# Conditional LoRA and paged attention in one kernel: a reordered prologue, and the last unit's probabilities transposed on TensorE

## What is computed

```python
w = weight[adapter_ids]; x = x + einsum('bsi,boi->bso', x, w)     # layer 0, per row
q, k, v = x @ Wq.T, x @ Wk.T, x @ Wv.T                            # 32, 8 and 8 heads of 128
q, k = rope(rmsnorm(q)), rope(rmsnorm(k))
k_all, v_all = concat(cache[block_table], new), 512 + 128 keys
probs = softmax(q @ k_all.T / sqrt(128), cached keys masked beyond cache_seqlens)
x = x + (probs @ v_all) @ Wo.T
```

## Time and profile before

| | us |
|---|---|
| median of 3 runs | 1047.99 (1045.32 to 1051.49) |
| the profiled execution | 1052.44 |
| its span in the trace | 1050.6 |
| TensorE busy in the span | 1013.0 (96%) |
| mean granted TensorE clock | 0.99 of full |

### The profile page before, as it was taken

How to read it: one execution, slowest core, us unless ns; L and a number is a source line. 1 busy time by engine, 2 the same in 40 slices (tenths; PEclk the granted TensorE clock), 3 DMA queues, 4 the chain that set the end, 5 groups by cost and what they waited for, 6 DMA issues and landing times.

```text
span 1050.6 us, 19559 instructions
## 1 busy us (share of the span) xinstructions
PE 1013.0 (96%) x5500; PEld 871.0 (83%) x5500; DVE 854.9 (81%) x1778; ACT 803.0 (76%) x2094; POOL 787.0 (75%) x807
## 2 busy tenths in 40 slices
PE   7789999999999999999999999999999999999996
PEld 5567878888888888888888888888888888888884
DVE  6556657666888898988989998898999989998893
ACT  4245546665788888898889888988888878988883
POOL 1767767565587978888888967888888968888663
PEclk9889999999999999999999999999999999999999
DMA  6679988888589889797888897798788988787874
GB/s 212 189 216 284 286 248 225 230 235 208 90 158 164 147 158 165 144 174 139 157 157 159 159 156 160 145 172 149 153 158 157 160 151 160 150 172 130 156 146 108
DMA packets 477501, 180.85 MB, mean 172 GB/s; under 512 B 420417, under 2 KB 457426, under 8 KB 475346
## 3 DMA queue, kind: packets, MB, share of 16 engines
q1 hardware_dynamic: 372480, 150.57, 68.8%
q10 hardware_dynamic: 103890, 26.94, 11.8%
q0 software_dynamic: 1024, 2.10, 0.7%
HBM read 109.25 MB, written 35.66 MB: 138 GB/s over the span
## 4 chain that ended last, share of the span: by engine, by line
PE 80%; SPq 4%; DVE 4%; ACT 3%; DMA 3%; POOL 3%; issue 3%; ACTq 0%; POOLq 0%; DVEq 0%
PE S L1226 19%; PE O L1159 6%; PE O L1161 6%; PE O L1160 6%; PE Q L1159 5%; PE Y L1159 5%; PE Q L1161 5%; PE Q L1160 5%; PE Y L1160 5%; PE Y L1161 5%; PE T L1165 4%; PE KV L1160 2%; PE KV L1161 2%; PE KV L1159 2%; SPq L394 2%
## 5 line engine op out<-in xcount | busy, mean ns | idle before, releaser
L945 DVE SCALAR_TENSOR_TENSOR pr<-pr,rc,raw 128x640 f16<-128x640 f32 x208 | 237.2, 1141 | 22.1 <-ACT raw L723 16.7
L925 DVE CUSTOM_DVE_ANT_0 pr<-S,mask,rst 128x640 f32<-128x640 f32 x256 | 225.3, 880 | 32.1 <-PE S L1226 27.8
L738 ACT ACTIVATE pr<-pr,nb 128x640 f32<-128x640 f32 x256 | 211.6, 827 | 25.1 <-DVE nb L925 25.1
L723 ACT ACTIVATE raw<-pr,rc 128x640 f16<-128x640 f32 x208 | 166.3, 825 | 3.2 <-DVE rc L941 2.9
L540 POOL TENSOR_TENSOR m<-m 128x512 f32<-128x512 f32 x64 | 111.3, 1739 | 71.3 <-DVE m L973 68.6
L494 POOL TENSOR_TENSOR kl<-raw,kh 128x512 fp32r<-128x512 f32 x64 | 96.6, 1509 | 47.8 <-ACT kh L622 47.2
L1226 PE MATMUL S<-kh,qh 128*128 128x320 f32 x512 | 121.4, 318 | 7.1 <-DVE nb L925 6.4
L682 ACT ACTIVATE Q<-Q 128x128 f32<-128x128 f32 x256 | 68.2, 267 | 73.5 <-DVE m L973 73.5
L515 POOL TENSOR_SCALAR ptl<-first 128x512 fp32r<-128x512 f16 x130 | 103.1, 793 | 23.0 <-DMA first<-pr 12.8
L515 POOL TENSOR_SCALAR ptl<-turned 128x512 fp32r<-128x512 f16 x130 | 102.8, 790 | 20.5 <-DMA turned<-pr 10.4
L1226 PE MATMUL S<-kh,ql 128*128 128x320 f32 x512 | 116.8, 309 | 0.0
(11 more groups left out here) (114 smaller groups left out, 2694.2 us busy)
## 6 DMA issues: line engine op xcount, KB each, us to landing
cache_rows<-in_kv SPq DMA_DIRECT2D x80, 256.0 KB, 4.9
wraw<-in_wall SPq DMA_DIRECT2D x73, 256.0 KB, 3.2
raw<-cache_rows SPq DMA_DIRECT2D x63, 256.0 KB, 3.2
raw<-cache_rows ACTq DMA_DIRECT2D x49, 256.0 KB, 4.1
cache_rows<-in_kv ACTq DMA_DIRECT2D x48, 256.0 KB
mask<-mask_rows SPq DMA_DIRECT2D x64, 128.0 KB
first<-in_lw SPq DMA_DIRECT2D x6, 1024.0 KB
acc<-in_x SPq DMA_DIRECT2D x8, 256.0 KB
```

The costliest lines, as they stand in the source:

```text
L723: e.activation(upper16[:, g, :], pr[:, slot(u, g), :], ACT.Copy, scale=rc[:, u % 2, g:g + 1]).then_inc(a_f1, 1)
L738: e.activation(pr[:, slot(u, g), :], pr[:, slot(u, g), :], ACT.Exp, bias=nb[:, u % 2, g:g + 1], scale=-1.0, accum_out=sm[:, u % 2, g:g + 1 ...
L925: e.tensor_tensor_reduce(pr[:, slot(u, g), :].rearrange("p (a n) -> p a n", a=2), S[:, :, 0:320], mask[:, u % 2, :].rearrange("p (a n) -> ...
L945: e.scalar_tensor_tensor(out=lower16(u, g), in0=pr[:, slot(u, g), :], scalar=rc[:, u % 2, g:g + 1], in1=upper16[:, g, :], op0=ALU.mult, op ...
```

## The change

In the prologue: 34 warm-up transposes for 44. SP loads row 1 in the middle of unit 0's key pages, and row 2 ahead of the mask; chunk 5 moves to ACT's queue, where all six chunk loads now stand behind the five small loads, and ACT also loads unit 1's first four key pages. POOL issues the four gathers of unit 0 before its loop, as DVE makes the page indices first. Unit 0's keys are split after its queries. L0 of row 1 is computed on PE in period -1, between the projections and turns of unit 0, its sum and transposition come at once, and `project_q(1)` follows two score products of unit 0; the other two are done at the places that they have in all later periods. DVE's four table parts move to the end of period 0. POOL's gathers of unit 1 all come after its `scales(1)`.

In the tail: unit 63's four probability tiles are normalised in place (two on ACT, two on DVE), turned by 20 transposes on PE into banks T, S and S, multiplied into bank Q (not O) and projected into bank KV (not Y). Its planes and its eight DMA transposes are gone, and PE's last part is written out as one list in which the two last units alternate. The semaphores' counts follow.

```diff
-N_WARM = 44
+N_WARM = 34
...
+        def turned_at(u, t):
+
+            if u == LAST:
+                return S[:, t - 2, :] if t in (2, 3) else T[:, t % 2, :]
+            return T[:, T_BANK[t], :]
...
             load_x(0)
-            for t in range(NT):
-                load_kt(0, t)
-            load_w(0, 5)
+            for t in range(2):
+                load_kt(e, kt_regs, 0, t)
+            load_x(1)
+            for t in range(2, NT):
+                load_kt(e, kt_regs, 0, t)
             e.wait_ge(c_rows, 1)
             e.dma_start(mask_rows, mask[0:NB, 1, 0:NT * P]).then_inc(d_rows, 16)
-            load_x(1)
+            load_x(2)
             e.wait_ge(d_rows, 16)
             load_mask(0)
             load_mask(1)
-            for t in range(NT):
-                load_kt(1, t)
-            load_x(2)
+            for t in range(1, NT):
+                load_kt(e, kt_regs, 1, t)
             for c in range(6, NWC):
                 load_w(0, c)
...
+                if i < LAST:
+                    turn_upper(i, 0)
                 if i < NU:
-                    turn_upper(i, 0)
                     load_v(i)
+                if i < LAST:
                     turn_lower(i, 0)
                     turn_upper(i, 1)
...
+            for t in range(NT):
+                gather_v(0, t)
...
-                if 0 < j < NL:
+                if 1 < j < NL:
                     gather_v(j, 0)
                     gather_v(j, 1)
-                keys_lo(j)
+                if i >= 0:
+                    keys_lo(j)
                 split_w(i, 0)
                 q_sum(j)
                 scales(j)
-                if i < 0:
-                    gather_v(0, 0)
-                    gather_v(0, 1)
-                if j < NL:
+                if i == -1:
+                    keys_lo(j)
+                if j == 1:
+                    gather_v(j, 0)
+                    gather_v(j, 1)
+                if 0 < j < NL:
                     gather_v(j, 2)
                     gather_v(j, 3)
...
-                for t in range(3):
-                    p_lo(w, t)
+                if w < LAST:
+                    for t in range(3):
+                        p_lo(w, t)
                 split_w(i, 1)
-                p_lo(w, 3)
-                p_lo(w, 4)
+                if w < LAST:
+                    p_lo(w, 3)
+                    p_lo(w, 4)
...
+                if u < NA or u == LAST:
+                    rounded(pth[:, i % 3, :], turned_at(u, t)).then_inc(a_p, 1)
...
+            def norm_last(g):
+                e.wait_ge(v_rc, 2 * LAST + 1)
+                e.activation(pr[:, slot(LAST, g), :], pr[:, slot(LAST, g), :], ACT.Copy,
+                             scale=rc[:, LAST % 2, g:g + 1]).then_inc(a_norm, 1)
...
-            for c in range(5):
-                e.dma_start(w_raw(0, c), wall[0, :, c * WC:(c + 1) * WC]).then_inc(d_w[c], 16)
...
                             table[g:g + 1, :].broadcast_to([32, NB * NT])).then_inc(d_tab, 16)
+            for c in range(6):
+                e.dma_start(w_raw(0, c), wall[0, :, c * WC:(c + 1) * WC]).then_inc(d_w[c], 16)
...
-            split_chunk(0, 0)
-            split_chunk(0, 1)
...
             e.activation(sn, ang, ACT.Sin).then_inc(c_sin, 1)
             e.wait_ge(c_ang, ANG_COS)
             e.activation(cs, rnd, ACT.Sin).then_inc(c_cos, 1)
+            split_chunk(0, 0)
+            split_chunk(0, 1)
+            l0_hi(0)
+            for c in range(2, 6):
+                split_chunk(0, c)
             e.wait_ge(c_cos, 1)
             e.activation(warmed[:, :], mhalf[:, :], ACT.Exp)
-            split_chunk(0, 2)
-            l0_hi(0)
-            split_chunk(0, 3)
-            split_chunk(0, 4)
-            split_chunk(0, 5)
+            e.wait_ge(d_page, 16)
+            load_kt(e, copy_regs[0:4], 1, 0)
...
                     output_hi(o)
+                if i == 0:
+                    l0_hi(1)
                 if real:
                     exp(i, 0)
                 for place in copied[0:2]:
                     copy_page(*place)
-                if i == 0:
-                    exp(0, 1)
-                    exp(0, 2)
-                keys_hi(j)
-                if i == 0:
-                    l0_hi(1)
-                    exp(0, 3)
+                if i >= 0:
+                    keys_hi(j)
                 if turn:
                     p_hi(w, 0)
...
                 new_v_hi(j)
-                if i > 0:
+                if real:
...
                 q_hi(j)
-                if i > 0:
+                if i == -1:
+                    keys_hi(j)
+                if real:
...
-                output_hi(o)
+                if w != LAST:
+                    output_hi(o)
...
-                if real:
+                if i < LAST:
                     upper_plane(i, 0)
+                elif i == LAST:
+                    norm_last(0)
+                    exp(i, 2)
+                    norm_last(1)
+                    exp(i, 3)
                 if turn:
                     p_hi(w, 0)
+                if w == LAST:
+                    output_hi(w - 1)
+                if turn:
                     p_hi(w, 1)
...
+                if i < LAST:
                     exp(i, 2)
...
+            def norm_last(g):
+                e.wait_ge(v_rc, 2 * LAST + 2)
+                e.tensor_scalar(pr[:, slot(LAST, g), :], pr[:, slot(LAST, g), :],
+                                rc[:, LAST % 2, g:g + 1], None, ALU.mult).then_inc(v_norm, 1)
...
+            key_rows()
+            l0_add(0)
             split_chunk(0, 0)
             split_chunk(0, 1)
+            l0_lo(0)
+            for c in range(2, 6):
+                split_chunk(0, c)
             for part in range(4):
                 rope_part(0, part, 0)
-            l0_add(0)
-            split_chunk(0, 2)
-            l0_lo(0)
-            for c in range(3, 6):
-                split_chunk(0, c)
-            key_rows()
...
                 if i >= 0:
                     largest(i, 0)
                 if i == 0:
-                    for g in range(1, G):
-                        largest(0, g)
-                    l0_add(1)
                     l0_lo(1)
-                    recip(0, slice(0, 3))
-                    recip(0, slice(3, 4))
-                    for part in range(4):
-                        rope_part(1, part, 1)
                 q_products(j)
                 if turn:
                     p_lo(w, 0)
-                if i > 0:
+                if i >= 0:
                     largest(i, 1)
                 if turn:
                     p_lo(w, 1)
...
-                if i > 0:
+                if i >= 0:
                     largest(i, 2)
...
-                if 0 < i < NA:
+                if 0 <= i < NA:
...
-                if i > 0:
+                if i >= 0:
                     largest(i, 3)
...
                 if i == -1:
+                    l0_add(1)
                     rope_part(0, 1, 1)
...
                     scaled_recip(i, 1)
+                if i == 0:
+                    for part in range(4):
+                        rope_part(1, part, 1)
...
                     largest(i, 1)
+                if w == LAST:
+                    p_lo(w, 0)
                 output_lo(o)
+                if w == LAST:
+                    for t in range(1, 5):
+                        p_lo(w, t)
...
+                if i < LAST:
+                    scaled_recip(i, 0)
+                elif i == LAST:
+                    recip(i, slice(0, 2))
                 if real:
...
-                if real:
+                if i < LAST:
                     lower_plane(i, 1)
+                elif i == LAST:
+                    recip(i, slice(2, 4))
+                    norm_last(2)
+                    norm_last(3)
                 add_output(o)
-                if real:
...
+            def turn_last(t):
+                if t == 0:
+                    e.wait_ge(a_norm, 2)
+                    e.wait_ge(v_norm, 2)
+                elif t == 1:
+                    e.wait_ge(v_q, NU)
+                elif t == 2:
+                    e.wait_ge(v_max, 4 * NU)
+                elif t == 4:
+                    e.wait_ge(v_p, 5 * NA + 1)
+                four_turned(turned_at(LAST, t),
+                            [pr[:, slot(LAST, g), t * P:(t + 1) * P] for g in range(G)]
+                            ).then_inc(p_t, 1)
+
...
-                    if u >= 1:
+                    if u == LAST:
+                        e.wait_ge(a_sqq, NU)
+                    elif u >= 1:
                         e.wait_ge(v_o, u)
...
                 if i == 0:
-                    for t in range(3):
-                        l0_part(1, t)
-                        scores(0, t + 1)
-                    l0_part(1, 3)
                     l0_turn(1)
+                    scores(0, 1)
...
                 project_kv(j)
-                if lb == 2:
-                    l0_product(lb)
+                if lb == 1:
```

(75 more changed lines are left out.)

50 lines of the change are left out of this document (28 added, 22 removed).

## The result

Over 20 runs of each kernel the median went from 1048.57 to 1039.95 us, a ratio of 0.992 with a 95% interval of 0.990 to 0.994: 8.6 us less. The forecast was 1035.5 in a range of 1031 to 1043. So the side and the range held, and the size was taken too large: 12.5 where 8.6 came. The forecast's own arm, 1033 to 1038, was missed; the measured median lies 0.55 us from the value of the rival "SP's queue sets the pace", 1040.5. The profiled execution took 1041.16 us, 11.3 less than the profiled 1052.44 of before.

What follows compares the result with a forecast made beforehand. PE, busy 96% of the span, was taken as the bound, with losses in the first 74 us and after the last scores. Prologue -10 and tail -2.5 give -12.5: median 1035.5 us, range 1031 to 1043.

Steps and rivals of the forecast that it cites:

- own arm: Whole kernel: the main forecast, median 1035.5 us with its own range 1033 to 1038, chance 0.60.
- SP's queue sets the pace: Prologue: key pages and loads of rows 3 to 5 come only 5 us earlier, PE waits; 1040.5 us, chance 0.17.
- First scores: Prologue, unit 0: first scores at 26.3 instead of 27.90, 1.6 us sooner; bounds no gain to 2.5.
- wrong: Signs against: waits for early chunks, row 1's matrix or loads at 70 to 110, low clock in row 0's L0, tail norm stop.
- slower: Prologue: row 1's matrix lands late and holds the turn and scores behind L0; 1053 us, chance 0.03.
- `project_q(1)`: Prologue, second row: starts 3.5 us after the first scores, at 29.8 instead of 40.11, 10.3 us earlier.
- `turn_q(2)`: Prologue, PE's next wait, before at 65.76: 53 by POOL's order (-12.7), or 56.3 to 56.5 by the gather (-9.3).
- SP's brake: Prologue: SP's queue gains four pages, chunk 5 and a wait, some 5 us at unit 3, against 10 us key slack.
- Prologue as a whole: All steps up to PE's gapless part: -10 us, ends -5 and -14.
- The clock: Prologue rival: the lower clock behind the stop goes too, -14 there; 1031.5 us in all, chance 0.08.
- Warm-up: Start: ten fewer transposes cost and gain nothing, covered by row 0's matrix load; at most 1.75 us if the clock fell.
- Tail: After the last scores: two PE stops go, 20 transposes add 2.2 us; -2.5 us, ends -1 and -3.5.

Runs made afterwards that it cites:

- the second profile: The unedited kernel before, profiled a second time; that execution took 1053.44 us.
- the run with three edits: Kernel after with mask rows stored early, SP's page copies moved behind row 4's loads, and period 2's weight chunks issued ahead of unit 4's keys; 0.9866 of before.
- the three runs with several edits of SP's list: Kernel after with early mask rows and early weight chunks, plus one of three orders of SP's page copies; 0.9866, 0.9886 and 0.9857 of before.
- the tail alone: Kernel before with only the tail part of the change, without the prologue part; 0.9977 of before, 2.4 us.
- L0 put back: Kernel after with row 1's L0 back between unit 0's score products, period 0's order on PE, DVE and ACT too, queues kept; 0.9970 of before.
- the early chunks alone: Kernel after with period 2's two weight chunks issued ahead of unit 4's 16 key pages on SP; 0.9904 of before.

## Why the forecast was right in side and too large in size

Two chains ran at once: PE's own (L0, scores, projection) and SP's list of loads. The change shortened the first by some 10 us and the second by less than was counted. The range held in part by luck: it was wide enough to take in the rival that the runs bear out.

- **First scores.** Forecast 26.3, measured 24.68: 3.2 us, past the upper bound of 2.5. ACT has no wait for a weight chunk there any more, which was the text's best case. The projections of unit 0 also ran in a window with a granted clock of 0.93 where it was 0.77, but that is the smaller part: the four profiles with the low clock there have 25.29 to 25.55, still ahead of the forecast. PE stopped 0.51 us for row 1's matrix, one of the signs named under "wrong", and not more, so the rival "slower" had no footing.
- **`project_q(1)`.** Forecast 29.8, measured 30.52. One wait was missing in the step: the first `largest` waited 1.59 us for the masks, which SP issued only once the store of the mask rows had landed.
- **`turn_q(2)`.** Forecast 53 or 56.3 to 56.5, measured 56.91. That is near the second value by luck, since that one had PE wait for the gather, and `values_hi(1)` began with no wait for it. POOL's own order came 3.9 us later than worked out (49.86 for 46). ACT's timeline of after, then POOL's:

```profile
35.43 0.63 ACT L650 ACTIVATE kh<-raw 128x512 fp32r<-128x512 f32 x1 [5.77 <-DMA raw<-in_kv]
```

```profile
37.38 1.26 POOL L561 TENSOR_TENSOR m<-m 128x512 f32<-128x512 f32 x1
...
44.29 0.95 POOL L507 DMA_INDIRECT raw<-in_kv,kidx  x1 [0.30 <-issue]
45.29 4.59 POOL L525 TENSOR_SCALAR pr<-pr,rc 128x640 f32<-128x640 f32 x4
49.86 0.62 POOL L546 TENSOR_SCALAR vh<-raw 128x512 fp32r<-128x512 f32 x1
```

  The projection of Q ran at a granted clock of 0.76 in 30 to 40, ACT stood 5.77 us for unit 1's keys, and the four norms took 4.59 us where 3.14 had been counted.
- **SP's brake, the step that failed.** The text gave SP 5 us at unit 3 and set that against 10 us of slack of the keys. In fact unit 3's key pages began at 55.26 on SP's queue where they had begun at 56.40. Row 4's matrix was issued at 70.57 (before 74.20, and 71.42 and 70.22 in the other two profiles with its prologue) and the chunks at 95.38 (99.65, 95.53 and 95.84): up to 4 us sooner than in the first profile, and next to nothing against the other two. The slack of the keys was real, but the matrix and the chunk in the same list had none; the earlier trace rows showed ACT waiting 2.20 us for that very chunk at 110, and the text named it and took -10 all the same. A faster prologue turned a wait of 2.20 (none in the second profile) into one of 3.56 to 10.08. The mechanism of the rival "SP's queue sets the pace" is what happened: it had -5 for the prologue and 1040.5 in all, measured -6.1 and 1039.95. That the loads behind SP's queue are what kept the rest back is shown by the run with three edits, which changes only SP's list (and which pages ACT copies) and gains 5.7. It was given 0.17 and deserved more. Of the signs named under "wrong" this one came too: new waits of ACT, for keys at 71.0 (0.52 us) and for the chunk at 102.5.
- **Prologue as a whole.** -10 forecast, -6.1 measured alone. In the three runs with several edits of SP's list unit 4 came at 109.80 to 110.03, 7.5 to 11.7 us ahead of the three profiles with the prologue of before. So the 10 are about what PE's side can give once SP's list lets it.
- **The clock.** The rival had it come back too. In the profiles it partly did: the shortfall of the granted clock times the window's length adds up to 8.5 us in 16 to 74 before (0.77 and 0.72 of the earlier trace rows, and 0.97 and 0.86 in 30 to 40 and 40 to 52: 13.85 x 0.23 + 10 x 0.03 + 12 x 0.14 + 12 x 0.28), 6.8 in the second profile and 3.4 after (13.85 x 0.07 + 10 x 0.24); an estimate, and an upper one, since PE idles in part of it. Worked out in the same way it is 5.2 for the tail alone, 6.8 with L0 put back, and 0 to 4.4 in the ten profiles with the new prologue. So the clock did come back in part, and its share of the 6.1 us was not separated. The low level is 1.2 GHz, half of the full 2.4. The runs with 44 warm-ups and with the early chunks alone had none in 16 to 74 and were no faster at unit 4 (114.14, 114.42).
- **Warm-up.** Forecast nothing, measured 0.5 us (44 slower) within an interval of +-2.9. L0 of row 0 took 3.67 us in all ten profiles with 34, so the 1.75 us, the price of that L0 at the low level, did not come. But "the cover is that load" held in six of the ten only: in four PE idled 1.38 to 1.63 us before it, and the clock was low at the next step, the projection of unit 0. The first scores came 0.4 to 1.1 us later there, which the wait for the masks took up. The prediction called the cut risky by the Trainium skill, "TensorE: Matmul & The Clock Gate", Part 1 (The HAM clock gate). The traces neither show nor exclude it, since the clock fell at that projection with 44 as well, in two profiles of four.
- **Tail.** -2.5 forecast, -2.4 measured. (42 matmuls at 0.23 are 9.7 and not 9.8, which changes nothing.) 12.4 us were worked out from the restart to the end of the last value product, 12.4 came (1019.34 to 1031.7). The restart, 0.4 and not 0.2 later against PE's place before, is ended by ACT's `p_hi(62, 0)` behind the exps and norms, and by POOL's `p_lo(62)`, which had waited 7.80 us for the lower planes' transposes; the two stops for `output_lo(62)` and for unit 63's transposes are gone.

## What to carry to other kernels

When one engine's chain is shortened by 10 us, ask of every load behind it, one by one, when it is issued and when it is first used: slack of the most frequent load says nothing about the others in the same in-order queue. A wait for a load that does not come sooner itself grows by what is gained ahead of it; one that is already in a trace, however small, is the first to look at. And where a stop only moves one unit on with each repair, open the gates together: each alone measured nothing to 1.7 us here, none clear of its interval of some 3, and the three together 5.7, which is.

## What was not expected of the hardware

- The masks, moved ahead on SP's queue while the DMA engines were 0.93 busy, landed no sooner: issued at 21.52 for 24.12, first used at 28.24 for 27.81. All five profiles with that edit have the first use at 27.76 to 28.84, the five with the same prologue and without it at 27.69 to 28.09, and in all ten it ends a wait for the masks. It is no rule, though: row 4's matrix, issued at 62.78 in the run with three edits and at 70.57 in the kernel after, came in time there, with the DMA engines 0.94 busy in 62 to 74.
- POOL's four norms took 4.59 us beside DVE's table parts and 3.14 without them. DVE's timeline beside them, then the line of the norms (min/median/max in ns of all 48 in the program):

```profile
46.11 3.11 DVE L923 SCALAR_TENSOR_TENSOR tab<-acc 128x384 f32<-128x384 f32 x4
```

```profile
L525 POOL TENSOR_SCALAR pr<-pr,rc x48: 791/802/1562, 45.3 to 251.7; 128x640 f32<-128x640 f32 x48
```

  The four norms beside the table parts took 0.810 us at least, 1.132 in the median and 1.562 at most, where the median of the 48 is 0.802; the four table parts took 0.545 to 1.155 us. The Trainium skill, "SBUF — State Buffer", section "SBUF: two separate sides", says that VectorE and GpSimd take the shared ports exclusively and that the loser waits out the whole instruction. The longest norm is longer by 0.76, which is within the lengths of one table part and agrees with it. But 1.45 us in all is about two table parts (3.11 / 4 = 0.78 in the mean) for four norms, so not each norm waited out a whole part. It goes either way, too: in the ten profiles with the new prologue the norms took 3.44 to 4.60 us and the table parts 2.57 to 3.99, where the norms alone took 3.13 to 3.14 in the four with the old order. In the tail POOL's five `p_lo(62)` took 3.66 us beside two DVE norms and 3.87 before, so there it cost nothing. The section names on VectorE's side instructions with two inputs in SBUF, which a table part has and a norm has not, or ones in a two-port mode. Whether the norms ran in such a mode no run here shows. The prediction had left that condition out when it priced the norms by the rule.
- The granted clock falls at other places in two executions of the same kernel (0.77 and 0.72 in 16 to 30 and 62 to 74 in one, 0.75 and 0.86 in the other). It was below 1.00 somewhere between 16 and 134 us in each of the 14 profiles here, with 34 warm-ups and with 44, so one profile says little of what a change did to it.
